# Attention stage: the query and key rows of a group are loaded in twelve DMAs of 16 rows instead of six of 48, 32 and 16 rows

## What is computed

```python
h = concatenate([tok, txt], axis=1)            # 4 x 640 x 512
h = h + attn(layernorm(h))
h = h + ffn(layernorm(h))                      # top 2 of 8 experts
# attn, on projected Q, K, V with 32 heads of 16 columns:
attn = einsum('bqhd,bkhd->bhqk', Q, K)
probs = softmax(attn, axis=-1)
ctx = einsum('bqhd,...', probs, V)             # then an output projection
```

## Time and profile before

| | us |
|---|---|
| median of 3 runs | 1917.68 (1916.17 to 1921.87) |
| the profiled execution | 1914.11 |
| its span, first to last instruction | 1912.3 |
| TensorE busy | 1396.4 |
| VectorE busy | 1304.3 |

### The profile page before, as it was taken

One profiled execution on the slowest core, in us unless ns is written; L12 is line 12 of the kernel. 1 busy time (PEld: TensorE's weight loads), 2 busy tenths in 40 slices (PEclk: granted clock), 3 DMA queues, 4 the chain that ended last, 5 costly groups with the idle time before them and its releaser, 6 DMA issues. The chain is left out here.

```text
span 1912.3 us, 29870 instructions
## 1 busy us (share of the span) xinstructions
PE 1396.4 (73%) x10126; PEld 786.8 (41%) x10245; DVE 1304.3 (68%) x2158; ACT 770.2 (40%) x1459; POOL 514.1 (27%) x325
## 2 busy tenths in 40 slices
PE   0375127734998989989999933458729999999993
PEld 0343103211433334334344410124517777777772
DVE  7975999975877877777888829776454444444441
ACT  4473103320766666666677730012203333333331
POOL 4000015661233333343310000234211233333321
PEclk9886558865999999999999976555559999999997
DMA  4002004664355455445432340101347888878865
GB/s 139 1 1 80 0 1 148 207 210 154 115 193 183 170 187 187 167 172 205 151 113 81 110 153 30 31 28 55 138 163 261 277 280 276 267 263 266 268 182 132
DMA packets 108067, 288.99 MB, mean 151 GB/s; under 512 B 14767, under 2 KB 49327, under 8 KB 97851
## 3 DMA queue, kind: packets, MB, share of 16 engines
q1 hardware_dynamic: 84354, 205.72, 30.3%
q0 software_dynamic: 22592, 79.70, 14.6%
q10 hardware_dynamic: 1056, 2.79, 0.5%
HBM read 201.17 MB, written 92.08 MB: 153 GB/s over the span
## 5 line engine op out<-in xcount | busy, mean ns | idle before, releaser
L1256 DVE TENSOR_REDUCE mxa<-p 128x1 f32<-128x512 f32 x640 | 410.4, 682 | 145.4 <-PE p L1166 145.2
L1282 ACT ACTIVATE pT<-p 128x512 f32<-128x512 f32 x800 | 424.1, 607 | 199.7 <-PE p L1184 125.2
L1166 PE MATMUL p<-ks,qs 96*128 96x512 bf16 x640 | 254.9, 401 | 87.0 <-DMA vs<-d_v 84.6
L1184 PE MATMUL p<-qs,ks 128*128 128x512 bf16 x560 | 217.0, 387 | 18.1 <-ACT pT L1282 11.9
L1202 PE MATMUL p<-pT,vs 128*32 128x128 f32 (+1 forms) x2560 | 209.2, 445 | 1.4 <-ACT pT L1282 1.4
L1787 PE MATMUL p<-x,w 128*128 128x256 bf16 x1728 | 191.6, 273 | 0.0
L1787 PEld LDWEIGHTS p<-x,w 128*128 128x128 bf16 x1728 | 169.0, 98 | 23.4
L1758 POOL DMA_INDIRECT d_acc<-yo,slot_row x54 | 86.9, 1609 | 312.5 <-DMA d_acc<-yo,slot_row 247.2
L1166 PEld LDWEIGHTS p<-ks,qs 96*128 96x128 bf16 x640 | 62.5, 98 | 195.4 <-DMA vs<-d_v 64.8
L1137 POOL CAST xT<-xT 128x2048 bf16<-128x2048 f32 x24 | 45.3, 1886 | 347.1 <-PE p L1202 336.2
L1866 DVE SCALAR_TENSOR_TENSOR sg<-p,b,sg 128x256 f32<-128x256 f32 x108 | 52.2, 484 | 121.9 <-ACT sg L1832 121.8
(11 more groups left out here) (335 smaller groups left out, 2190.1 us busy)
## 6 DMA issues: line engine op xcount, KB each, us to landing
w<-d_w SPq DMA_DIRECT2D x18, 2048.0 KB, 8.5
d_w<-xT POOLq DMA_DIRECT2D x24, 1024.0 KB, 9.6
shared<-d_w SPq DMA_DIRECT2D x9, 2048.0 KB
w<-d_w SPq DMA_DIRECT2D x18, 1024.0 KB, 7.2
xT<-in_w1T POOLq DMA_DIRECT2D x16, 1024.0 KB, 14.6
d_v<-xT SPq DMA_DIRECT2D x20, 512.0 KB, 4.4
vs<-d_v SPq DMA_DIRECT2D x32, 320.0 KB
d_o<-osb SPq DMA_DIRECT2D x32, 320.0 KB, 4.7
```

Source lines behind the costliest of these rows:

```text
L1166: mm = pe.matmul(out, qs[u][0:STACK, h, q], ks[u][0:STACK, h, 0:512], start=True, stop=True)
L1184: mm = pe.matmul(out, ks[u][:, h, k], qs[u][:, h, 0:512], start=True, stop=True)
L1256: dve.tensor_reduce(mxa[u][:, h, qt:qt + 1], bank, AX.X, ALU.max, negate=True).then_inc(s_mfree, 1)
L1282: act.activation(dst, ps[:, second_bank(c, s)], ACT.Exp).then_inc(s_p, 1)
```

## The change

Every 16-row block of `qs` and of `ks` gets a DMA of its own. Before, the Q part 0 was read once and spread over three blocks by a broadcast, and the three K parts beside it were one DMA of 48 rows; the second pair of DMAs had 32 rows, the third 16. The bytes that reach `qs`, `ks` and `vs` and their places are the same, and so are all other engines' instructions. The value that TensorE waits for goes from 16 x 7 to 16 x 13 per load.

```diff
-    RUNS = [(0, 3, 0), (3, 2, 1), (5, 1, 2)]
-    LOADS = 2 * len(RUNS) + 1
+    PARTS = [(0, 0), (0, 1), (0, 2), (1, 0), (1, 1), (2, 0)]
+    LOADS = 2 * len(PARTS) + 1
...
-                for at, n_parts, part in RUNS:
-                    part_rows = slice(at * HD, (at + n_parts) * HD)
-                    q_part, k_parts = (src.rearrange("s (c h) t -> s c (h t)", h=GH) for src in (
-                        d_q[part:part + 1, bass.ds(rows, GH * HD)], d_k[0:n_parts, bass.ds(rows, GH * HD)]))
-                    sp.dma_start(qs[u][part_rows].rearrange("p h t -> p (h t)"),
-                                 q_part.broadcast_to([n_parts, HD, GH * T])).then_inc(s_ld[u], 16)
-                    sp.dma_start(ks[u][part_rows].rearrange("p h t -> p (h t)"), k_parts).then_inc(s_ld[u], 16)
+                for at, (q_part, k_part) in enumerate(PARTS):
+                    part_rows = slice(at * HD, (at + 1) * HD)
+                    for dst, src, part in ((qs, d_q, q_part), (ks, d_k, k_part)):
+                        sp.dma_start(dst[u][part_rows].rearrange("p h t -> p (h t)"),
+                                     src[part, bass.ds(rows, GH * HD)].rearrange("(c h) t -> c (h t)", h=GH)
+                                     ).then_inc(s_ld[u], 16)
```

## The result

| | before | after |
|---|---|---|
| median of 4 runs, us | 1918.11 (1916.17 to 1921.87) | 1868.28 (1865.57 to 1872.1) |
| profiled execution, us | 1914.11 | 1869.23 |
| span, us | 1912.3 | 1867.4 |

The ratio is 0.9739, with a 95% interval of 0.9716 to 0.9763, that is 49.8 us between the medians.

A forecast was written before the change was run, and what follows sets the result against it. The prediction took loads passing through few DMA engines, which TensorE waits for, as the bound. 16.0 + 5.7 + 37.0 + 1.1 = 59.8 us took the profiled 1914.1 to 1854.3, the median to 1858; range 1849 to 1884.

The forecast's parts named there:

- The start: Attention stage's first load: first matmul at 432.5 instead of 448.5, 16.0 us saved, bounds 17.9 and 12.1.
- The second group's wait: At the attention stage's start, TensorE's second wait for a load goes: 5.7 us saved, lower bound 3.
- the sooner rise: TensorE's clock, 0.50 up to 481 us, could reach 1.00 sooner without waits; range put 3 us lower for it.
- The 23 intervals: Loop, between stores of the context: each falls from 20.61 to 19.0 us, 37.0 us saved, bounds 40.7 and 25.5.
- what would be late next: Loop: the wait for the maximum row, up to 1.0 us, late in most periods; interval 19.5, gain 25.5 us.
- Cost 0: SP's issue of a load takes 1.9 us more, 6.4 against 4.6, but nothing waits for SP behind it.
- floor of 18.84: Loop: shortest interval expected, from three intervals without a load wait; below it nothing to gain.
- The rest: After the 23 intervals: the last slow interval falls from 19.91 to 18.84, 1.1 us; later ones and other stages keep their lengths.
- The first: Rival, in the loop: the maximum row or the exponentials take over at a period of 19.8; 1876 us, chance 0.10.
- The second: Rival, in the loop: memory or all engines together are the bound, 20.5 us a group; 1895 us, chance 0.07.
- The third: Rival: one load's DMAs complete in sequence, 3.0 us each, period 31.6; 2215 us, slower ones 0.05 together.
- The fourth: Rival: rows of `d_q` and `d_k` are slow whatever DMA carries them; no change, 1917.7 us, chance 0.04.

The follow-up runs named there:

- e1: Kernel before the change, its six Q and K DMAs kept but with the 16 head columns as outer dimension; 1849.48 us, ratio 0.9656.
- e3: Changed kernel, its twelve Q and K DMAs kept but read with an outer dimension of 2; 2048.19 us.
- e4: Changed kernel, its twelve Q and K DMAs kept but read with an outer dimension of 4; 1867.38 us.
- E7: Changed kernel with the maximum row's DMA issued two slots earlier; 1857.69 us, ratio 0.9697.
- e8: Changed kernel with GpSimd's two 1 MB transfers of a group started two values steps later; 1854.90 us, ratio 0.9684.
- six16: The kernel of e1: six Q and K DMAs as before the change, with outer dimension 16; 1849.48 us, ratio 0.9656.
- e6: Kernel before the change with only K split into six DMAs of 16 rows, Q in its three of before; 1879.79 us.
- e5: six16 with each group's load in the loop held until 11 more scores of the group; 1925.76 us, ratio 1.005.

## Why the prediction was right, and where its terms were off

**The cause** is shown: a load passed through few engines, and the change spreads it over 16. Experiments e1, e3 and e4 separate that from the number and size of the DMAs, and their DMA shares and packet counts give the number of engines. The share of 0.17 under a full queue was the row that told it. The prediction's 320 KB on the first two engines left out their shares of the other DMAs (10 KB of the 16-row blocks, 20 KB of V), while its 80 KB after the change has them in; like for like it is 350 KB against 80. Nothing in the sum uses it.

**The start.** Forecast 16.0 for the first group, measured 14.7: the first matmul at 433.76, 5.2 us after the last DMA of the load had been issued and 0.4 behind the range of 431.4 to 433.4 that I gave. The second group's wait went, but the 5.7 us did not all arrive: the new wait of 3.24 us for the maximum row took more than half. Up to the first second-pass matmul the two terms gave 479.11 - 461.88 = 17.2 us of 21.7. From there to the first store it took 486.19 - 461.88 = 24.3 us against 501.83 - 479.11 = 22.7, so 15.6 us stand at the first store. Most of the 1.6 us more are TensorE's clock (the third column from the end), after the change and then before it:

```profile
466.00:468.00 2.00, 2.00 (x6) 0.60 (x4) 1.66 (x3) 1.48 (x3) 0.00 (x0) 0.50 0.57 214
468.00:470.00 2.00, 2.00 (x20) 0.63 (x19) 0.69 (x1) 0.91 (x2) 0.00 (x0) 0.93 0.00 0
...
482.00:484.00 2.00, 2.00 (x10) 0.81 (x8) 1.84 (x3) 1.61 (x4) 0.00 (x0) 0.73 0.72 195
```

The clock rose at about 468.3 instead of 483.1 us, worked out from these means. That is 15 us sooner in the span, but 6.4 us behind the first second-pass matmul instead of 4.0: 2.4 us more at half the clock cost 1.2 us, by this estimate. The wait of 3.24 us stands just before this stretch, 0.39 before. So the sooner rise for which I had allowed 3 us gave nothing beyond the two terms.

**The 23 intervals.** Forecast 19.0 us each and 37.0 in all, measured 19.42 and 27.4. This is the term that was mis-sized. I had named what would be late next and taken it into the bound (19.5, 25.5 us) but not into the value; the measured gain lies near that bound. The step that failed is "Cost 0" for the issue time: 7.7 us a load in the loop instead of 6.4, and those DMAs run into the row's. That my check of the cover looked only at who waits for SP, and not at who shares the DMA engines, is the lesson. E7, e8 and e1 show the difference to be this wait: with 2.2 us of it or none the 23 intervals are 18.79, 18.70 and 18.73 us on average. The stores of e1 that bound them:

```profile
481.78 0.38 SPq L1088 DMA_DIRECT2D d_o<-osb  x1
...
912.63 0.38 SPq L1088 DMA_DIRECT2D d_o<-osb  x1
```

Against e1 the changed kernel loses 23 x (19.42 - 18.73) = 15.9 us, and it waits 16.6 us for the row. The prediction's floor of 18.84 was also a little high: the intervals of e1 repeat as 18.5, 18.9, 18.9 and 18.6, and three intervals in a row can miss a short one.

**The rest.** From the 24th store to the last it is 144.75 us against 145.31, 0.6 where 1.1 was forecast; 1.3 us are gained in other stages, without a cause that I looked for. The sum is 15.6 + 27.4 + 0.6 + 1.3 = 44.9, where 59.8 was forecast for the profiled execution. The medians moved by 49.8, so the median after was 10 us above the 1858 and inside the range.

**The rivals.** The first was right in kind, a part of its size: the maximum row did take over, at a period of 19.42 and not 19.8. The second, all engines or the memory as the bound, falls: six16 runs the loop at 18.73 us a group with the same bytes. The third, DMAs in sequence, falls with a landing 5.2 us after the last of 13 issues; with it falls the Trainium skill's advice to join small transfers as a reason for a slower kernel. The 2.2 us per DMA of the prediction came from a fit that its page "DMA: Bandwidth & Descriptors" states for DMAs issued by GpSimd (SWDGE), and these were issued by SyncE. The advice is right in a milder way: seven DMAs beat thirteen by 19 us once both use all engines, though 13 of these come back by moving GpSimd's transfers (e8), with thirteen DMAs. The fourth falls with the result.

**Left open.** Why 5 KB need 7 to 10 us beside a load and GpSimd's transfers, and why e6 starts so late. Who is served first in the engines, or how deep their queues are, was not measured. A run without GpSimd's transfers was not tried.

## What to carry to other kernels

When a DMA queue is backed up while the DMA share is low, multiply the share by 16: it gave 2.7 engines here before the change, 1.9 and 3.8 with outer dimensions of 2 and 4. If the number is small, look at the outer dimension of the DMAs. Reorder the dimensions so that 16 is outermost, as six16 does, before you cut the transfer into more pieces; where a sum runs over partitions, their order is free and makes that possible. Then look at the small, urgent DMAs beside it: once the load spread over all engines here, its moment of issue decided whether a 5 KB transfer was late.

## What the runs showed of the hardware that was not expected

- With the same bytes, SP's queue took 35.7% of the engines' time instead of 30.3%, and the DMA share at the start read 1.04 at 177 to 219 GB/s, where 253 GB/s went with a share of 0.68 before. A share near 1 is so no measure of bandwidth by itself.
- Delaying a load by about 3 us (e5), with no engine waiting for it, made the kernel 76 us slower than e1, through a 5 KB transfer that was used 9.8 us after its issue in the case shown, and through TensorE's clock, which fell to 0.50 in that wait.
